# A shorter front chain and a paired tail in a two-layer RWKV and mixture-of-experts tower

## The reference, cut to what matters

```
h = h + moe0(norm(h))                   # 8 dense-run experts 256->1024->256, top 2 by gates: "dense units"
xn = layernorm(h);  k, r = xn@Wk, xn@Wr # second layer's time mix
y  = wkv_scan(w, u, k, r)               # stable recurrence along the sequence
h2 = h + (sigmoid(r) * y) @ Wo
x  = layernorm(h2)                      # then the attention block
q, k, v = rms(x)*n1 @ wq, wk, wv        # 16 heads of 16; rms of each head of q and k
ao = softmax(q k^T / 4, causal) v @ wo ;  x = x + ao
y  = rms(x)                             # router over 4 experts, top 2
h  = h2 + x + w0*e0(y) + w1*e1(y) + w2*e2(y) + w3*e3(y)
# e0: gelu, down; e1: silu(y w1)*(y w2), down; e2: gelu l1, gelu l2, gelu l3, l4; e3: gelu down, gelu up, out
```

## Time and profile before

| | us |
|---|---|
| median of 3 runs | 3387.07 |
| the runs | 3387.07, 3381.96, 3387.25 |
| profiled execution, its own time | 3385.92 |
| its span, first to last instruction | 3384.1 |
| PE busy | 2812.2 (83%) |
| ACT busy | 1785.9 (53%) |
| DVE busy | 1691.8 (50%) |
| POOL busy | 1391.0 (41%) |
| mean granted clock of TensorE | 0.941 |

### The profile page before, as it was taken

The page is one execution under the profiler, slowest core; times in us unless marked ns, Lnnn a source line. Parts: engine busy times, 40 slices in busy tenths (PEclk is TensorE's granted clock), DMA queues, the critical chain, the costliest instruction groups (busy, mean ns, idle before and its releaser), DMA issues. The chain is left out here.

```text
span 3384.1 us, 58992 instructions
## 1 busy us (share of the span) xinstructions
PE 2812.2 (83%) x21872; PEld 1878.7 (56%) x22208; DVE 1691.8 (50%) x3163; ACT 1785.9 (53%) x2817; POOL 1391.0 (41%) x1326
## 2 busy tenths in 40 slices
PE   3778776896888998899879987998799879985678
PEld 2445454564665666566646664666466646662455
DVE  6777745526346443644364436443544455445452
ACT  2535344555555565555555655565556555653433
POOL 5445433343344344434434443444334433442224
PEclk8999988999998999999999998999899989997889
DMA  1000007731121212222212121222121122211002
GB/s 64 13 19 19 12 13 269 269 119 50 63 80 57 77 68 71 72 82 76 79 56 83 68 87 56 83 68 74 68 83 68 68 72 79 74 51 38 27 27 64
DMA packets 62641, 242.58 MB, mean 72 GB/s; under 512 B 6784, under 2 KB 26528, under 8 KB 43552
## 3 DMA queue, kind: packets, MB, share of 16 engines
q1 hardware_dynamic: 60832, 234.69, 19.7%
q0 software_dynamic: 1536, 4.20, 0.4%
HBM read 207.13 MB, written 31.72 MB: 71 GB/s over the span
## 5 line engine op out<-in xcount | busy, mean ns | idle before, releaser
L1326 POOL TENSOR_TENSOR c_lo<-c_g,c_hi 128x512 bf16<-128x512 f32 x720 | 873.1, 1218 | 1580.1 <-ACT c_hi L1488 1407.7
L2151 PE MATMUL c_up<-c_xT,c_ring 128*128 128x512 bf16 x2877 | 720.5, 385 | 88.0 <-ACT c_hi L1488 31.7
L2168 PE MATMUL c_down<-c_ring,c_hi 128*128 128x256 bf16 x4096 | 718.0, 275 | 0.0
L1487 ACT ACTIVATE c_g<-c_up,b 128x512 f32<-128x512 f32 x512 | 353.3, 690 | 525.0 <-PE c_up L2151 492.9
L2168 PE MATMUL c_down<-c_ring,c_lo 128*128 128x256 bf16 x2048 | 564.4, 276 | 0.0
L2151 PEld LDWEIGHTS c_up<-c_xT,c_ring 128*128 128x128 bf16 x3072 | 294.0, 99 | 365.2 <-ACT c_hi L1488 39.6
L2168 PEld LDWEIGHTS c_down<-c_ring,c_hi 128*128 128x128 bf16 x4096 | 399.2, 99 | 113.1 <-issue 1.6
L1488 ACT ACTIVATE c_hi<-c_up,b 128x512 bf16<-128x512 f32 x512 | 350.7, 685 | 0.0
L1487 ACT ACTIVATE c_g<-c_up 128x512 f32<-128x512 f32 x176 | 106.2, 603 | 357.1 <-PE c_up L1917 356.7
L1754 DVE CAST c_room<-c_room 128x384 bf16<-128x384 f32 x256 | 146.0, 610 | 275.3 <-PE c_front L2063 260.9
L2168 PEld LDWEIGHTS c_down<-c_ring,c_lo 128*128 128x128 bf16 x2048 | 202.3, 99 | 25.3
(11 more groups left out here) (324 smaller groups left out, 5439.5 us busy)
## 6 DMA issues: line engine op xcount, KB each, us to landing
c_ring<-kept_dense SPq DMA_DIRECT2D x112, 1024.0 KB, 4.8
c_ring<-kept_experts SPq DMA_DIRECT2D x72, 512.0 KB, 3.3
c_room<-in_WB SPq DMA_DIRECT2D x16, 1024.0 KB, 7.4
kept_dense<-c_ring SPq DMA_DIRECT2D x16, 1024.0 KB, 4.9
c_ring<-kept_experts SPq DMA_DIRECT2D x32, 384.0 KB, 3.4
kept_experts<-c_room SPq DMA_DIRECT2D x9, 512.0 KB, 3.8
c_xT<-kept_xT SPq DMA_DIRECT2D x8, 512.0 KB, 4.1
out<-h SPq DMA_DIRECT2D x8, 512.0 KB, 4.4
```

Of the source, the lines that this page charges most:

```text
L1326: pool.tensor_tensor(lo14[:, a, :], g[:, h % 4, :], hi14[:, a, :], ALU.subtract).then_inc(lo_ready.sem, 1)
L1487: act.activation(g[:, h % 4, :], ub[n % 2][:, :], ACT.Gelu, bias=bias)
L2151: last = pe.matmul(ub[n % 2][:, :], r[:, wp, o + q * P:o + (q + 1) * P], xT[:, xp, q, :], start=(m == 0 and q == 0), stop=(m == 2 and q == ...
L2168: m = pe.matmul(bank, (hi14, lo14)[xp][:, a, s * P:(s + 1) * P], r[:, wp, o + KC * P:o + CHUNK], start=False, stop=(k == HC0 - 1 and n == ...
```

## The change

1. **Order string.** New numbers, and Zx0 moves ahead of A1. `Q0 Q1` come back to back, then `Qx0 Qx1`. The maxima are three steps a sequence with four groups each. W becomes Wa (heads 0 and 1 of four) and Wb (heads 2 and 3), Wa ahead of V.
2. **Four banks.** Blocks of odd number take their q, k and v in fb[0] and fb[1] (`qkv_banks`), and their stacks in fb[2] and fb[3] (`stack_banks`); the maxima go round all four.
3. **Low halves last** in four products (Wo, wo, r1, and q and k with their own wait): `low_last` does the high halves of all blocks, waits for the low half, then the low ones.
4. **Plan.** One more up unit around each group's start; expert units at new places; `held` puts two D behind a G.
5. **Tail.** Iteration 7 has no expert units (`PLAN_B`); iteration 8 has those of tiles 5 and 6 as pairs (`PLAN_CC`), with places in `hi14` and `lo14` for y and the router weights of tile 6 (`y_parts`, `wt_late`), `first_tile` says which tile an iteration's experts start with; the loop is iterations 3 to 6.

```diff
@@ orders
-        tokens += ["Sa%d" % n, "E%d" % n, "+1.3", "Sb%d" % n, "+2.6"]
+        tokens += ["Sa%d" % n, "E%d" % n, "+2.6", "Sb%d" % n, "Wa%d" % n, "+2.6"]
         if q:
             tokens.append("V%d" % (n - 1))
-        tokens += ["W%d" % n, "+3.9"]
+        tokens += ["Wb%d" % n, "+3"]
...
-    return " ".join("m%d +2" % (b * 6 + q) for q in range(6))
+    return " ".join("m%d +1.5" % (b * 3 + q) for q in range(3))
...
-    return ("Q%d +1.3 Qx%d +2 Q%d +1.3 Qx%d +2 X%d K%d +5 T%d +1.3 Tx%d K%d +5 T%d +1.3 Tx%d +1.5"
-            % (s, s, r, r, b, s, s, s, r, r, r))
+    return ("Q%d Q%d +1.3 Qx%d Qx%d +3.5 X%d +1.3 K%d +5 T%d Tx%d K%d +4 T%d Tx%d +3"
+            % (s, r, s, r, b, s, s, s, r, r, r))
...
-    "f0 +3 r2x r2 +3 f1 +2.5 f1x +3 f2 +3 f2x A0 +7 Rx0 Ra0 +3 Rb0 +4 Rc0 A1 +6 Zx0 Z0 +5 Rx1 Ra1 +3 Rb1 +4 Rc1 +5 Zx1 Z1",
-    "+2 f5 +2 f5d +6 g5 +4 f6 +2 f6x +3", keys_order(0), maxima_order(0), "j0 +2 N0 +1 Nx0 +1.5", heads_order(0),
-    "+2 O0 +1", keys_order(1), maxima_order(1), "j1 +2 N1 +1 Nx1 +1.5", heads_order(1),
-    "+2 O1 +2 f13 +2 f13x +3 g13 +2 b0 +6 y0 +1 b1 +2 b1x +3 r1 +1.5")).split()
+    "f0 +5 r2x r2 +8 f1 +2.5 f1x +3 f2 +3 f2x A0 +8 Rx0 +3 Ra0 +3.5 Rb0 +6 Rc0 +5 Zx0 A1 +7 Z0 Rx1 +3 Ra1 +3.5 Rb1 +6 Rc1 +4 Zx1 Z1",
+    "+2 f5 +3 f5d +6 g5 +4 f6 +2 f6x +3.5", keys_order(0), maxima_order(0), "j0 +2 N0 +1 Nx0 +1.5", heads_order(0),
+    "+1.5 O0 +1", keys_order(1), maxima_order(1), "j1 +2 N1 +1 Nx1 +1.5", heads_order(1),
+    "+1.5 O1 +3 f13 +2 f13x +3 g13 +2 b0 +6 y0 +1 b1 +2 b1x +4 r1 +1.5")).split()
@@ plan
+PAIR = [("e2_l1", 0), ("e2_l1", 1), ("e2_l2", 0), ("e2_l2", 1), ("e2_l3", 0), ("e2_l3", 1), ("e0_up", 0), ("e2_l4", 0),
+        ("e0_up", 1), ("e2_l4", 1), ("e3_down", 0), ("e0_down", 0), ("e3_down", 1), ("e0_down", 1), ("e3_up", 0),
+        ("e3_up", 1), ("e1", 0), ("e3_out", 0), ("e1", 1), ("e3_out", 1), ("e1_down", 0), ("e1_down", 1)]
...
+        between = {8: ["more", "e0_down", l2[0]], 16: [l3[0]], 24: [d3[0], "e2_l4", d3[1]], 32: [u3[0]],
+                   40: [g1[0], "e3_out", g1[1]], 48: [g1[2]], 56: ["more", "e1_down"]}
+        after = {9: l2[1], 11: l2[2], 13: l2[3], 18: l3[1], 20: l3[2], 22: l3[3], 34: u3[1], 36: u3[2], 38: u3[3]}
+        ahead = {51: g1[3]}
+    held = 0
     for d in range(NB):
...
+        held = max(held - 1, 0)
+        if not held:
+            plan += ups(d + LAG + 1)
+        for u in between.get(d, ()):
+            plan += c_units(u) if u in DOWNS else ups(d + LAG + 2) if u == "more" else [u]
+        if d in ahead:
+            plan.append(ahead[d])
+        if plan[-1][0] == "G":
+            held = 2
+        elif d and d % HC0 == 0:
+            plan += ups(d + LAG + (3 if "more" in between.get(d, ()) else 2))
         plan.append(("D", d))
@@ run
-            with eng.Fori(3, TILES) as i:
+            with eng.Fori(3, TILES - 1) as i:
                 go(ORDER_BC, dense(i, PLAN_BC, PLAN_BC), front(i - 1), gates(i - 2))
-            go(ORDER_C, dense(TILES, PLAN_C, PLAN_BC), front(TILES - 1), gates(TILES - 2))
-            go(["r2x", "r2"] + PLAN_C.units, dense(TILES + 1, PLAN_C, PLAN_C), gates(TILES - 1))
+            go(ORDER_B, dense(TILES - 1, PLAN_B, PLAN_BC), front(TILES - 2), gates(LATE))
+            go(ORDER_CC, dense(TILES, PLAN_CC, PLAN_B), front(TILES - 1), gates(TILES - 2))
+            go(["r2x", "r2"] + PLAN_C.units, dense(TILES + 1, PLAN_C, PLAN_CC), gates(TILES - 1))
+
+        def stack_banks(s):
+            return fb[2 * (s % 2):2 * (s % 2) + 2]
+
+        def qkv_banks(s):
+            return fb[2 - 2 * (s % 2):4 - 2 * (s % 2)]
@@ PE
+            def low_last(name, n, lo_wait, ready):
+                for low in range(2):
+                    if low:
+                        pe.wait_ge(*lo_wait)
+                    for s in range(SUB):
+                        o = fb[2 + s // 2][:, (s % 2) * D:(s % 2) * D + n]
+                        for wp, xp in PARTS[2:] if low else PARTS[:2]:
+                            for k in range(KC):
+                                m = pe.matmul(o, X[xp][:, k, s * P:(s + 1) * P], W(wp, name, k, 0, n),
...
-                        for n in (2 * half, 2 * half + 1):
+                        for n in range(4 * third, 4 * third + 4):
                             m = b * 12 + n
-                            if n >= 2:
-                                pe.wait_ge(mx_ready.sem, mx_ready.at(t, m - 1))
-                            bank = fb[n % 2]
+                            if n >= 4:
+                                pe.wait_ge(mx_ready.sem, mx_ready.at(t, m - 3))
+                            bank = fb[n % 4]
```

More of the change, by code:

```diff
@@ L817, in make_plan, with ups @@
     if not dense:
-        for name in ("e2_l1", "e0_up", "e2_l2", "e0_down", "e3_down", "e2_l3", "e3_up", "e2_l4", "e1", "e3_out", "e1_down"):
-            plan += c_units(name)
-        return plan
-    boundary, after = {}, {}
+        for name, j in ONE if experts == 1 else PAIR:
+            plan += c_units(name, j)
+        return plan
+    def ups(n):
+        return [("U", u) for u in range(sum(x[0] == "U" for x in plan), min(n, NB))]
+    between, after, ahead = {}, {}, {}
     if experts:
         plan += c_units("e2_l1") + c_units("e0_up")
[L824 to L829, removed]
-    for d in range(NB):
[L831 to L835, removed]
-            plan.append(("U", ups))
-            ups += 1
+        l2, l3, d3, u3, g1 = (c_units(name) for name in ("e2_l2", "e2_l3", "e3_down", "e3_up", "e1"))
+        between = {8: ["more", "e0_down", l2[0]], 16: [l3[0]], 24: [d3[0], "e2_l4", d3[1]], 32: [u3[0]],
[3 more added lines that the diff above has]
+    held = 0
+    for d in range(NB):
+        held = max(held - 1, 0)
[9 more added lines that the diff above has]
+            plan += ups(d + LAG + (3 if "more" in between.get(d, ()) else 2))
         plan.append(("D", d))
@@ L1018, in phase_bc, with mixing @@
                   for j in range(2))
-        lg, pr, wt = (rest[:, 2 * SUB * E1 * E1 + j * SUB * E1:2 * SUB * E1 * E1 + (j + 1) * SUB * E1]
-                      .rearrange("p (s e) -> p s e", s=SUB) for j in range(3))
+        lg, pr, wt, wt_late, real = (rest[:, 2 * SUB * E1 * E1 + j * SUB * E1:2 * SUB * E1 * E1 + (j + 1) * SUB * E1]
+                                     .rearrange("p (s e) -> p s e", s=SUB) for j in range(5))
+        def mixing(t):
+            return wt_late if isinstance(t, int) and t == TILES - 2 else wt
         r1s = sb("r1", [P, 4, SUB])
@@ L1092, in piece_done @@
             if u[0] == "O":
-                return dn1.sem, dn1.at(i, plan.group["c", u[1]] + 1)
+                return dn1.sem, dn1.at(i, plan.group["c", u[1], u[3]] + 1)
             return up_ps.sem, up_ps.at(i, plan.up[u] + (2 if u[0] == "G" else 1))
@@ L1112, in slot_of @@
                 return 8 + u[1] % 6
-            return plan.home["e1" if u[0] == "G" else u[1]] + u[-1]
+            return plan.home["e1" if u[0] == "G" else u[1], u[-1]] + u[-2]
         def tokens_of(i, plan, step):
@@ L1122, in phase_bc @@
             ORDER_0.append(u)
-        ORDER_B, ORDER_BC, ORDER_C = (plan.braid(ORDER_F) for plan in (PLAN_B, PLAN_BC, PLAN_C))
+        ORDER_B, ORDER_BC, ORDER_CC = (plan.braid(ORDER_F) for plan in (PLAN_B, PLAN_BC, PLAN_CC))
+        for order, last in ((ORDER_BC, ("G", HC - 1, 0)), (ORDER_CC, ("G", HC - 1, 0))):
+            assert order.index(last) < order.index("b1")
         def go(order, *stages):
@@ L1298, in low, with low_weights @@
                     return f
-                def low_weights(q):
+                def low_weights(q, half):
                     def f():
-                        for n in range(q * GROUP, (q + 1) * GROUP):
+                        for n in range(q * GROUP + half * 2, q * GROUP + half * 2 + 2):
                             if n % HEADS % 3 == 2:
@@ L1721, in f @@
                     def f():
-                        for n in (2 * q, 2 * q + 1):
+                        for n in range(4 * q, 4 * q + 4):
                             m = b * 12 + n
@@ L1746, in negatives, with high_weights @@
                     return f
-                def high_weights(q):
+                def high_weights(q, half):
                     def f():
-                        for n in range(q * GROUP, (q + 1) * GROUP):
+                        for n in range(q * GROUP + half * 2, q * GROUP + half * 2 + 2):
                             dve.wait_ge(p_f.sem, p_f.at(t, n + 1))
@@ L1871, in r2 @@
                 def r2():
-                    E.begin(t)
+                    wt = mixing(t)
+                    if not (isinstance(t, int) and t == TILES - 2):
+                        E.begin(t)
                     dve.wait_ge(lg_exp.sem, lg_exp.at(t))
@@ L1919, in feature_major, with token_major @@
                 return m
-            def token_major(o, name, s, xs, n):
+            def token_major(o, name, s, xs, n, lo_wait):
                 for j, (wp, xp) in enumerate(PARTS):
```

(3 more changed lines are left out.)

192 lines of the change are left out of this document (106 added, 86 removed).

## The result

The changed kernel takes 3221.26 us (median of four runs, 3216.66 to 3225.03) against 3387.16; the ratio is 0.9513, with a 95% interval from 0.9496 to 0.9529. The forecast was 3226. The profiled execution has a span of 3220.4 us at a mean clock of 0.959 (before 3384.1 and 0.941). Of all executions in this text, one of the kernel with +3 in front of f1 (3708.72 us) and one of the kernel before that ran beside it (4877.85 us) were in a slow state, at granted clocks of 0.741 and 0.555, and count in no figure.

A forecast was written before the change was run, and what follows sets the result against it. Full iterations were bound by PE's in-order work plus about 40 us idle, iterations 1 and 8 by the front's chain. Terms -75, -24, -66 and +5 gave -160 from 3385.9: 3226 us, range 3150 to 3310.

The forecast's parts named there:

- B: Full iterations: ACT's detours and DVE's moved steps give back all 15 us, only tail and iteration 1 gain; 3301, chance 0.14.
- C: Head groups: ACT kept from Gelu costs 3.0 us more in each of 64 groups, +192; 3418, chance 0.11.
- D: Tail: the second tile's experts fill no wait, so iteration 8 takes 315 us; 3286, chance 0.05.
- A: Full iterations: old waits go and no new ones come, 11.6 us more in each of five; 3168, chance 0.19.
- the clock's 3.4: Full iteration: two stretches of PE work at granted clock 0.57 return to full clock, saving 3.4 us.
- Start: Front's start: 8 us more cover ends f1's wait for `xn` (-6.2); the router's table loads cost 2.4.
- Accumulator: Expert's first down unit: DVE empties the previous group earlier, so the 8.3 us wait falls by 5.9 to 2.4.
- Gated units: Expert units: two down units behind each gated unit take back 3.3 of PE's 5.3 us wait for `g`.
- Heads: Head groups, full iteration: doubled cover removes Sb's 5.1 us wait on ACT; ACT's detours cost 4.4.
- Rival E: Recurrence's second half: Rb1's two-input DVE operations meet POOL, costing 2.9 us in each of five iterations; 3240, chance 0.11.
- Maxima: Maxima stage: four banks cut a block's 14.1 us to 8 to 9; -10 in iteration 1, nothing directly in full iterations.
- 0.44 us for each us of added units: Tail, iteration 8: 65 us more expert units add 29 us, less 24 for the shorter front: +5, 255 us.

## Why the prediction was right, and where it wasn't

**The frame held, and two misses cancelled.** Full iterations were to lose 15 us each and lost 17.4; iteration 1 was to be 270 and is 272; iteration 7 270 and is 270; iterations 8 and 9 were to be 327 and are 336. So the full iterations gave 12 us more than forecast, and the tail and iteration 1 some 11 less: that the total lies within 5 us of 3226 is in part luck. Rivals B, C, D and A are out by the same lines: no full iteration near 341 or under 315, no 3.3 us lost in a head group, iteration 8 under 300.

**Inside a full iteration the terms were off both ways.** PE's idle time fell 13.0 us (worked out: 11.9), its busy time 4.0 (the clock's 3.4). The clock's term was right in size and wrong in place. These are the stretches at the lower level around the end of the accumulator's wait, first of the kernel before (the wait ends at 2101.0), then of the changed one (it ends at 2019.2):

```profile
2097.90:2104.70 6.80, 3.67 (x24) 3.45 (x25) 6.73 (x13) 2.00 (x2) 0.00 (x0) 0.50 0.00 0
```

```profile
2019.40:2022.80 3.40, 3.40 (x24) 3.09 (x23) 3.40 (x3) 0.00 (x0) 0.00 (x0) 0.50 0.00 0
```

PE did 3.7 us of its work at that level there and does 3.4 now, so nearly nothing came back at this place; the window of the earlier trace rows, with its 0.57, began 4 us before the wait's end. The iteration had four such stretches, from 2046.7, 2097.9, 2330.0 and 2374.4, with 15.4 us of PE's work in them, and has two, from 2019.4 and 2183.2, with 6.9. If at most half of that time is lost, the gain is at most 4.3 us (an estimate from these sums).

- Start: the new wait at the router's table load is 2.46 us, worked out 2.4, and the wait of 6.2 is gone. That this is a net gain was the wrong entry: with the old numbers in the new front, PE waits 6.3 us at the start in three places (2.4, 2.5, 1.5) and the iteration is 7 us shorter. "8 us more of cover end that" came true, and the step that failed is that the cover was free. The order's numbers sum to 243.3 instead of 236.3 with it, so that every other gap gets 3% fewer units. I had priced the wait that the units cover and not the ones from which they were taken. Whether the thinner gaps or the new places of the units cost the 43 us is not shown.
- Accumulator: 4.8 left, not 2.4. The taking began 24.4 us after f2's end (1993.95 to 2018.32; worked out 23.0): 0.95 of these 1.4 us are a further operation of Rb0, L1696, which ran at 1.63 instead of 0.68 beside POOL, and Rb0 began some 0.5 later. PE was there after 20.5 us, not 21.4. The sign "under 3" failed with it.
- Gated units: 0 left, not 2.0. Norm after the recurrence: 0.2, not 1.2. `vh`: 0 left of 1.9, as worked out (the stacks wait 1.2, before 1.3); the router: 0.4 left of 1.1.
- Heads: 1.7 left before Sb instead of 0; up units behind the table loads 1.94 twice, 3.9, worked out 4.4. Up units in the key stage: 1.2 behind ACT's copies of Q2 and Q3, and 2.7 at G0 behind the table loads, 3.9 where 1.9 stood before; worked out 3.0 on top. All waits of up units for ACT rose by 7.7 us (4.2 to 11.9); 2.4, 4.4 and 3.0 are 9.8.
- Rival E: the meeting with POOL happened, three operations of Rb1 at 1.5 to 1.65. Its 2.9 us cost PE nothing visible in the second half: at f5 behind it the waits show 0.3 us. The sign that I gave for the forecast (0.69 there) was wrong, the time right.
- Maxima: 9.4 us with the emptying of 1.4 among them, 8 without; worked out 8 to 9.

**The tail's size.** The failed term is 0.44 us for each us of added units, read between iterations 8 and 1 before. The two pairs of kernels with and without the tail give 39 and 37 us for 65, 0.6 and 0.57. Two points that differ in what they lack (iteration 1 lacks experts, iteration 8 dense units) don't make a slope. With the new front, the second tile's experts raise PE's busy time in iteration 8 from 152 to 210 us, and its idle time falls from 75 to 56 only. The wait at f5 was filled, as I had said, 18.6 us without them and 4.1 with them; but the up units wait longer for ACT, first without the second tile's experts, then with them:

```profile
PE c_up L1968 <- ACT c_hi L1539: 5.9, 2, 4.3
```

```profile
PE c_up L1973 <- ACT c_hi L1543: 14.9, 6, 5.5
```

That experts depend on each other layer by layer fits this; no run separates it. The shorter front's 24 there is right (250 to 227).

**The parts don't add up.** Undone one at a time they cost 28 (tail), 59 (plan), 51 (maxima), 91 (keys), 26 (low halves), 9 (heads), 0 (weight copies) and -43 (start): 221 us, where all together are worth 166. I gave the maxima nothing in a full iteration (6.4 measured), and the key stage 1.9 less 3.0 (14). The 91 holds the order and the numbers of that stage too. The forecast came out right since the sum over the waits' rows is bounded by PE's 40 idle us and the sizes of its parts erred both ways, which is luck, not since each was known.

## What to carry to other kernels

When an in-order engine is full and other work is threaded through it, a cover of n units in one place is taken from every other gap; price the places that lose it, not only the wait that it ends, and expect a wait removed at one place to come back in smaller pieces (4.8 us at the accumulator did, with 6 parts more cover ahead of it). Try first what frees the dependent chain (more banks, fewer round trips): the maxima's two more banks were worth 3 to 8 us in every iteration, and the new query and key stage, banks and order together, 3 to 15, while the numbers of the order string changed sign from one iteration, and from one start of the chain, to the other. A part that leans on another, such as the paired tail on the short front (8 us alone, 28 with it), is to be timed with it.

## What the runs showed of the hardware

An operation on DVE took 1.5 to 1.65 us while POOL worked and 0.68 when it didn't, the same line both ways (L1696 above, 1.63 in the first half and 0.68 in the second). POOL worked from 2011.72 to 2017.85 in the first half, where L1696 began at 2016.76, and from 2041.73 to 2046.31 in the second, where it began at 2046.78. The Trainium skill (SBUF — State Buffer, Who interferes with whom) has the rule, that a VectorE instruction with two SBUF inputs contends with a GpSimd one that reads SBUF, and the trace agrees; what the runs add is that the slower operations stood ahead of the taking for which PE waited 4.8 us in one half, and ahead of a wait of 0.3 us in the other.

Each turn of the hardware loop shows as a wait of PE for nothing but "issue", 2.4 to 3.0 us in the changed kernel and its variants, and 1.2 to 2.2 in the kernel before and in the one with the new tail alone. The name alone doesn't prove it: with +3 in front of f1, iteration 1 has such a wait of 3.8 to 4.3 us at the transposes, in one case ending at 731.03, right behind DVE's norm (730.82), and iteration 8 of the kernel before has one of 2.9. Iteration 6 was 5.5 and 7.6 us shorter in the two pairs in which it lost the turn behind it; since the iteration behind it had other units too, how much of this is the turn's is not shown.
